# Seven-unit periods and a shared ring of banks in the attention stage of a two-layer fp32 kernel

## The reference, cut to what matters

```
q = _l2norm(q) * sm                 # sm = exp(min(scale_mul, log 100))
k = _l2norm(k)
scores = einsum('bhqd,bhkd->bhqk', q, k)
probs  = softmax(scores, axis=-1)
o      = einsum('bhqk,bhkd->bhqd', probs, v)
```

## Time and profile before

| what | us |
|---|---|
| three executions | 3588.06, 3583.96, 3587.75 |
| their median | 3587.75 |
| the profiled execution's own time | 3590.18 |
| span of the profiled execution, first to last instruction | 3588.4 |
| TensorE busy in the span | 3326.5 (93%) |
| VectorE, ScalarE, GpSimd busy | 2822.5, 2745.9, 2487.8 |
| granted TensorE clock, mean | 0.961 of full |

### The profile page before, as it was taken

One profiled execution on the slowest core, in us unless ns is written; L12 is line 12 of the kernel. 1 busy time (PEld: TensorE's weight loads), 2 busy tenths in 40 slices (PEclk: granted clock), 3 DMA queues, 4 the chain that ended last, 5 costly groups with the idle time before them and its releaser, 6 DMA issues.

```text
span 3588.4 us, 68227 instructions
## 1 busy us (share of the span) xinstructions
PE 3326.5 (93%) x22944; PEld 2607.0 (73%) x22944; DVE 2822.5 (79%) x2989; ACT 2745.9 (77%) x4725; POOL 2487.8 (69%) x1103
## 2 busy tenths in 40 slices
PE   7999999989799999997979999999798999999888
PEld 5778888864487888885357888888536888888643
DVE  2899999956299999994539999999445999999662
ACT  1989999933499999991449999998146999999523
POOL 1789999940098999992019999999103999999500
PEclk9999999998999999998889999999879999999989
DMA  3211212200112111110011111211002212111000
GB/s 125 86 61 54 69 54 67 66 24 1 51 60 67 57 66 61 60 66 12 1 63 60 61 62 61 66 56 60 12 1 74 65 55 65 54 60 54 24 12 6
DMA packets 56733, 186.83 MB, mean 52 GB/s; under 512 B 6577, under 2 KB 12721, under 8 KB 55473
## 3 DMA queue, kind: packets, MB, share of 16 engines
q1 hardware_dynamic: 56370, 182.26, 15.1%
HBM read 179.08 MB, written 3.16 MB: 51 GB/s over the span
## 4 chain that ended last, share of the span: by engine, by line
POOL 46%; PE 25%; issue 24%; DVE 3%; DMA 1%; ACT 0%; POOLq 0%; SPq 0%; DVEq 0%; ACTq 0%
POOL states L502 44%; PE bank L951 5%; PE bank L836 3%; PE bank L827 2%; PE bank L972 2%; PE bank L876 2%; PE bank L983 2%; PE bank L1025 2%; PE bank L828 1%; PE bank L750 1%; PE bank L776 1%; POOL part L485 1%; PE bank L939 1%; DVE states L1177 0%; PE bank L920 0%
## 5 line engine op out<-in xcount | busy, mean ns | idle before, releaser
L502 POOL TENSOR_TENSOR states<-states,c_rows 128x1024 f32<-128x1024 f32 x1024 | 2401.7, 2381 | 614.4 <-DMA c_rows<-c_spill 322.0
L1177 DVE TENSOR_TENSOR_SCAN states<-decay,bank 128x512 f32<-128x512 f32 x2048 | 2337.7, 1201 | 151.3 <-PE bank L828 105.7
L614 ACT ACTIVATE decay<-dt,a_log 128x512 f32<-128x512 f32 x2048 | 1305.9, 711 | 0.0
L836 PE MATMUL bank<-ident,states 128*128 128x128 f32 x8192 | 1240.5, 275 | 36.5 <-POOL states L502 13.0
L827 PE MATMUL bank<-ident,inflow_tok 128*128 128x128 f32 x6144 | 1068.7, 283 | 63.8 <-DVE states L1177 55.2
L608 ACT ACTIVATE inflow_tok<-dtx_tok,b_tok 128x512 f32<-128x512 f32 x1536 | 995.7, 713 | 134.3 <-PE bank L828 133.9
L836 PEld LDWEIGHTS bank<-ident,states 128*128 128x128 f32 x8192 | 952.4, 142 | 80.0 <-POOL states L502 77.5
L827 PEld LDWEIGHTS bank<-ident,inflow_tok 128*128 128x128 f32 x6144 | 687.5, 141 | 358.8 <-issue 126.0
L828 PE MATMUL bank<-b_diag,dtx_tok 128*128 128x128 f32 x4096 | 794.4, 276 | 0.0
L828 PEld LDWEIGHTS bank<-b_diag,dtx_tok 128*128 128x128 f32 x4096 | 621.1, 192 | 0.0
L1264 DVE TENSOR_REDUCE decay<-bank 128x1 f32<-128x512 f32 x256 | 166.4, 687 | 87.7 <-PE bank L951 86.6
(11 more groups left out here) (142 smaller groups left out, 1988.3 us busy)
## 6 DMA issues: line engine op xcount, KB each, us to landing
c_rows<-c_spill SPq DMA_DIRECT2D x256, 512.0 KB, 3.7
xproj_w<-in_xproj_w SPq DMA_DIRECT2D x32, 320.0 KB, 4.4
in_w<-in_in_w SPq DMA_DIRECT2D x16, 512.0 KB, 4.6
in_w<-in_fc_w SPq DMA_DIRECT2D x8, 512.0 KB, 5.3
xproj_w<-in_w SPq DMA_DIRECT2D x8, 512.0 KB, 5.0
xproj_w<-in_fc_w SPq DMA_DIRECT2D x4, 1024.0 KB, 4.7
y_gated<-in_mod_w SPq DMA_DIRECT2D x1, 2048.0 KB, 7.5
x_ahead<-in_x SPq DMA_DIRECT2D x4, 512.0 KB, 5.3
```

What stands on the lines that cost most here:

```text
L502: pool.tensor_tensor(pair, pair, c_row, ALU.mult).then_inc(weighed, 1)
L614: act.activation(decay[:, r % SLOTS * KI + k, :], dt[:, d, k, :], ACT.Exp, scale=a_neg[:, d, k, s:s + 1]).then_inc(decay_ready, 1)
L836: last = pe.matmul(banks[KI + t][:, k * P:(k + 1) * P], states[:, r % SLOTS * KI + k, t * P:(t + 1) * P], ident[:], is_transpose=True, sta ...
L1177: dve.tensor_tensor_scan(states[:, slot, time], decay[:, slot, time], banks[k % INFLOW_BANKS][:, time], 0.0, ALU.mult, ALU.add).then_inc(s ...
```

## The change

The stream is cut into 16 periods of four transposed units. In each of the first 11 periods three score units are woven in, in the order S T S T S T T, then comes the `weigh` of the period before, then at most one turn. The lead is 31 score units over seven banks (0 to 6). After the lead, score units go around banks 0 to 2 and transposed units around banks 3 to 6. The turned maxima and lanes no longer have a bank: each takes one slot in the ring of banks 0 to 2 in its turn (the first turn of maxima, inside the lead, uses bank 7). The copies of the turned maxima of groups 1 to 3 move from ScalarE to VectorE. `t_head` picks the head of a transposed unit so that neighbours again lie in different quarters. Nothing else in the program is changed, and the count of matmuls, reductions and exponentials is the same.

```diff
-LEAD = 22
+LEAD = 31
+LEAD_BANKS = 7
 S_BANKS = 3
-T_BANKS = 3
+T_BANKS = HG
+S_STEP = 3
+PERIODS = UNITS // HG
+S_PERIODS = (UNITS - LEAD) // S_STEP
+Q_MAX_PERIOD = {HG * g - 2: g for g in range(1, NG)}
+LANES_PERIOD = {HG * (g + 1) + 1: g for g in range(NG - 1)}
+TURN_PERIODS = sorted(list(Q_MAX_PERIOD) + list(LANES_PERIOD)) + [PERIODS]
...
+        def lead_last(bank):
+            return max(u for u in range(LEAD) if u % LEAD_BANKS == bank)
+        def score_slot(u):
+            n = u - LEAD
+            return n + sum(p < n // S_STEP for p in TURN_PERIODS)
+        def turn_slot(p):
+            return min(p + 1, S_PERIODS) * S_STEP + TURN_PERIODS.index(p)
+        def score_bank(u):
+            return banks[u % LEAD_BANKS] if u < LEAD else banks[score_slot(u) % S_BANKS]
+        def turn_bank(p):
+            return banks[turn_slot(p) % S_BANKS]
+        def t_head(v):
+            return (LEAD + v // HG * S_STEP + 2 + v % HG) % HG
...
-                q_max(0)
+                act.wait_ge(q_max_turned, b * NG + 1)
+                act.activation(q_t[:, 0, :], banks[7], ACT.Copy).then_inc(q_max_ready, 1)
...
-                    if g and at == HG:
+                    if g and at == HG - 1:
                         lanes(g - 1)
-                    if g + 1 < NG and at == STEPS - 3:
-                        q_max(g + 1)
...
+                def slot_free(x):
+                    if x < S_BANKS:
+                        pe.wait_ge(neg_ready, b * UNITS + lead_last(x) + 1)
+                        return
+                    owner = x - S_BANKS
+                    for k, p in enumerate(TURN_PERIODS):
+                        if turn_slot(p) == owner:
+                            if p in Q_MAX_PERIOD:
+                                pe.wait_ge(q_max_ready, b * NG + Q_MAX_PERIOD[p] + 1)
+                            else:
+                                pe.wait_ge(o_ready, b * NG + LANES_PERIOD[p] + 1)
+                            return
+                    for u in range(LEAD, UNITS):
+                        if score_slot(u) == owner:
+                            pe.wait_ge(neg_ready, b * UNITS + u + 1)
...
                 def scores(u):
-                    if u >= S_BANKS:
-                        pe.wait_ge(neg_ready, b * UNITS + u - S_BANKS + 1)
+                    if u >= LEAD:
+                        slot_free(score_slot(u))
+                    elif u >= LEAD_BANKS:
+                        pe.wait_ge(neg_ready, b * UNITS + u - LEAD_BANKS + 1)
...
                 def scores_t(v):
-                    g, kt, i = v // STEPS, v % STEPS // HG, v % HG
+                    g, kt, i = v // STEPS, v % STEPS // HG, t_head(v)
                     if v % STEPS == 0:
                         pe.wait_ge(q_max_ready, b * NG + g + 1)
-                    if v >= T_BANKS:
+                    if v < T_BANKS:
+                        pe.wait_ge(neg_ready, b * UNITS + lead_last(S_BANKS + v) + 1)
+                    else:
                         pe.wait_ge(probs_t_ready, b * UNITS + v - T_BANKS + 1)
...
                 for u in range(LEAD):
                     scores(u)
-                    if u == STEPS + S_BANKS - 1:
-                        turn_q_max(0)
-                for v in range(UNITS):
-                    if v + LEAD < UNITS:
-                        scores(v + LEAD)
-                    scores_t(v)
-                    g, at = v // STEPS, v % STEPS
-                    if v >= 2 * HG - 1 and v % HG == HG - 1:
-                        weigh((v - HG) // STEPS, (v - HG) % STEPS // HG)
-                    if g and at == STEPS // 2:
-                        turn_lanes(g - 1)
-                    if g + 1 < NG and at == STEPS - 3:
-                        turn_q_max(g + 1)
-                weigh(NG - 1, TT - 1)
-                turn_lanes(NG - 1)
+                    if u == STEPS + LEAD_BANKS - 1:
+                        turn_q_max(0, banks[7])
+                for j in range(PERIODS):
+                    v, u = j * HG, LEAD + j * S_STEP
+                    if j < S_PERIODS:
+                        scores(u)
+                        scores_t(v)
+                        scores(u + 1)
+                        scores_t(v + 1)
+                        scores(u + 2)
+                    else:
+                        scores_t(v)
+                        scores_t(v + 1)
+                    scores_t(v + 2)
+                    scores_t(v + 3)
+                    if j:
+                        weigh(j - 1)
+                    if j in TURN_PERIODS:
+                        slot_free(turn_slot(j))
+                        if j in Q_MAX_PERIOD:
+                            turn_q_max(Q_MAX_PERIOD[j], turn_bank(j))
+                        else:
+                            turn_lanes(LANES_PERIOD[j], turn_bank(j))
+                weigh(PERIODS - 1)
+                slot_free(turn_slot(PERIODS))
+                turn_lanes(NG - 1, turn_bank(PERIODS))
...
-                for u in range(UNITS):
+                for u in range(LEAD):
                     least(u)
-                    if u >= LEAD and (u - LEAD) // STEPS and (u - LEAD) % STEPS == STEPS // 2:
-                        divide((u - LEAD) // STEPS - 1)
-                for g in range(2, NG):
-                    divide(g)
+                for j in range(PERIODS):
+                    if j < S_PERIODS:
+                        for m in range(S_STEP):
+                            least(LEAD + j * S_STEP + m)
+                    if j in Q_MAX_PERIOD:
+                        g = Q_MAX_PERIOD[j]
+                        dve.wait_ge(q_max_turned, b * NG + g + 1)
+                        dve.tensor_copy(q_t[:, g, :], turn_bank(j)).then_inc(q_max_ready, 1)
+                    if j in LANES_PERIOD:
+                        divide(LANES_PERIOD[j], turn_bank(j))
+                divide(NG - 1, turn_bank(PERIODS))
```

More of the change, by code:

```diff
@@ L650, in batch @@
                     act.activation(to, banks[i], ACT.Copy).then_inc(qk_t_ready, 1)
-                def q_max(g):
-                    act.wait_ge(q_max_turned, b * NG + g + 1)
-                    act.activation(q_t[:, g, :], banks[6], ACT.Copy).then_inc(q_max_ready, 1)
                 def lanes(g):
@@ L945, in scores @@
                 def scores(u):
                     t, g, i = u % STEPS // HG, u // STEPS, u % HG
-                    if u >= S_BANKS:
-                        pe.wait_ge(neg_ready, b * UNITS + u - S_BANKS + 1)
+                    if u >= LEAD:
+                        slot_free(score_slot(u))
+                    elif u >= LEAD_BANKS:
+                        pe.wait_ge(neg_ready, b * UNITS + u - LEAD_BANKS + 1)
                     a = slice(i * LANE, (i + 1) * LANE)
-                    pe.matmul(banks[u % S_BANKS], q_t[a, g, t * P:(t + 1) * P], k_t[a, g, :], start=True,
+                    pe.matmul(score_bank(u), q_t[a, g, t * P:(t + 1) * P], k_t[a, g, :], start=True,
@@ L952, in scores, with turn_q_max @@
                               stop=True).then_inc(scores_mm, 1)
-                def turn_q_max(g):
+                def turn_q_max(g, to):
                     pe.wait_ge(neg_ready, b * UNITS + (g + 1) * STEPS)
-                    if g >= 2:
-                        pe.wait_ge(o_ready, b * NG + g - 1)
                     for t in range(TT):
-                        last = pe.transpose(banks[6][:, t * P:(t + 1) * P], qk_pad[:, t, g, :], ident[:])
+                        last = pe.transpose(to[:, t * P:(t + 1) * P], qk_pad[:, t, g, :], ident[:])
@@ L973, in scores_t, with weigh, turn_lanes @@
                               stop=True).then_inc(scores_t_mm, 1)
-                def weigh(g, kt):
-                    v = g * STEPS + kt * HG
-                    pe.wait_ge(probs_t_ready, b * UNITS + v + HG)
+                def weigh(j):
+                    g, kt = j // TT, j % TT
+                    pe.wait_ge(probs_t_ready, b * UNITS + (j + 1) * HG)
                     if g and kt == 0:
                         pe.wait_ge(lanes_ready, b * NG + g)
-                    for i in range(HG):
+                    for v in range(j * HG, (j + 1) * HG):
+                        i = t_head(v)
                         last = pe.matmul(banks[7][i * LANE:(i + 1) * LANE, :], v_ones[:, kt, g * HG + i, :],
-                                         probs_t[(v + i) % len(probs_t)], start=(kt == 0),
+                                         probs_t[v % len(probs_t)], start=(kt == 0),
                                          stop=(kt == TT - 1), tile_position=(0, i * LANE))
                     last.then_inc(pv_mm, 1)
-                def turn_lanes(g):
+                def turn_lanes(g, to):
                     pe.wait_ge(lanes_ready, b * NG + g + 1)
-                    if g == NG - 1:
-                        pe.wait_ge(o_ready, b * NG + g)
                     for t in range(TT):
-                        last = pe.transpose(banks[6][:, t * P:(t + 1) * P], o_lanes[:, g, t * P:(t + 1) * P], ident[:])
```

(7 more changed lines are left out.)

## The result

Four executions of the changed kernel have a median of 3529.15 us, four of the kernel before 3587.9. One of the changed kernel's four took 4454.76 us, at a mean granted clock of 0.674 where the others had 0.963 to 0.964; the other three lie between 3528.44 and 3529.55, and the ratio is theirs. It is 0.9835, with a 95% interval from 0.9822 to 0.9848: faster by some 59 us, against a forecast of 3532 (3518 to 3558). The profiled execution took 3529.55 us, its span is 3527.8.

What follows compares the result with a forecast made beforehand. Bank round trips were taken to bound the attention stage. 19.0 us to the loop plus 53.0 made 72.0 a stage, gaining 59.7, or 55.4 with one late clock fall: 3534.8 from 3590.2, so 3532 as median; range 3518 to 3558.

Steps and rivals of the forecast that it cites:

- The bound: Attention stage of the kernel before: the round trip of three banks (matmul, read, matmul) bounds it; loop period 3.98 us.
- Lead: First reduction to loop start: VectorE becomes the bound at 0.65 us a reduction; 19.0 us, nine score units more.
- TensorE is units ahead: Inside the lead: the reason why `turn_q_max(0)` and the exponential's table load would cost nothing.
- Periods 0 and 1: Loop start at half clock: period 0 takes 4.5 us, period 1 takes 0.6 above a warm one.
- Warm periods: Periods 1 to 10: seven units in two rounds, 1.95 us, plus `weigh` 1.00; 2.95 us each if no bank is late.
- third-round rival: Scored periods: a late score slot or row quarter forces a third round; 3573 us, half of it 3552; chance 0.08.
- rival of dearer rounds: Scored periods: each of the two rounds takes 0.3 us longer, 24 us in all; 3556 us; chance 0.06.
- Turns: Ends of periods 2, 5, 6, 9 and 10: four transposes each, 0.59 us, 3.0 us a stage.
- wait at the end of period 10: Turn of group 3's maxima needs the reduction of that period's own last score unit: 0.2 us.
- Periods 11 to 15: Transposed units only: periods alternate between 2.06 and 3.34 us, 12.9 in all; last `weigh` waits 1.3, takes 1.0.
- late fall: Section behind the score units: one clock fall to 1.2 GHz kept among the four stages, giving 4.3 us back.
- slower rival: Periods 1 to 10: the clock falls, a period takes 5.8 us; 3648 us with all ten cold; chance 0.04.

Runs made afterwards that it cites:

- e3: The changed kernel with three banks for the transposed units instead of four, order and turns unchanged: 3614.0 us.
- e2: The changed kernel with three banks instead of seven in its lead of 31 units (first turn moved too): 3567.5 us.
- e1: The kernel before with its lead of 22 score units over seven banks (first turn moved too), loop unchanged: 3574.7 us, ratio 0.9962 to the kernel before.
- e9: The kernel before with six banks instead of three for transposed units in the 22 steps without score units: 3582.3 us, ratio 0.9984.
- e4: The changed kernel with transposed unit v on head v mod 4, so neighbours often share a row quarter: 3541.2 us.
- e7: The changed kernel with seven filler matmuls (128 x 512, never read) in the lead's first 21 units, one behind every third: 3528.4 us.
- e10: The changed kernel with the order S S S T T T T in a period instead of S T S T S T T: 3547.3 us.
- e12: e11 with a filler matmul (128 x 512, never read) behind every fourth score unit of the lead: 3505.3 us, ratio 0.9773.
- e11: The changed kernel with a lead of 28, its turn at the end, twelve scored periods, six banks for transposed units behind them: 3517.1 us, ratio 0.9807.

## Why the prediction was right, point by point

**The bound.** The bank round trips were the bound. e3 gives one of them back and the gain is gone; e2 gives back another and 38 us of 59 are gone. In the kernel before, two of the three parts taken singly bring only 14 us (e1) and 6 us (e9), with falls of the clock against them.

**Lead.** Forecast 19.0 us from the first reduction to the loop, measured 18.7. Two terms were off and nearly cancelled: a reduction costs 0.60 in an unbroken row (13.84 for 23), not 0.65, and `turn_q_max(0)` was costed at nothing but costs the gap of 1.02. "TensorE is units ahead" was true of its stream, not of the array: the score units issued before the turn last until 848.12, the turn runs from 848.05 to 849.16 at half clock, and the next score unit starts at 849.10.

```profile
835.18 12.94 PE L993 MATMUL bank<-dtx_tok,dt 32*128 32x512 f32 x46 [0.78 <-DVE dtx_tok L1306]
848.05 1.11 PE L1000 MATMUL bank<-ident,decay 128*128 128x128 f32 x4
849.10 4.92 PE L993 MATMUL bank<-dtx_tok,dt 32*128 32x512 f32 x16
```

That the sum came out within 0.3 us is luck.

**Periods 0 and 1.** From the first loop unit to the first `weigh` forecast 4.5 + 2.55, measured 6.9 (854.94 to 861.83). The clock was back 24.6 us after the first reduction, as before (24.6).

**Warm periods.** 2.95 forecast, 2.92 measured. Two rounds for seven units, with no bank late, even behind turns. The third-round rival did not occur; e4 shows that it would have, by 0.84 in four periods, with other heads, and by the wait that the rival names: the turned slot with its slack of 0.2 us. The rival of dearer rounds falls with the 1.92 us of seven units, and with it the Trainium skill's factor of 3.07 (TensorE: Matmul & The Clock Gate, Part 3): here four units cost the time of one.

**Turns.** 0.59 each: from 864.75 to 868.26 is 3.51 = 2.92 + 0.59. The wait at the end of period 10 is 0.16 (890.49 + 1.00 to 891.65), forecast 0.2.

**Periods 11 to 15.** From `weigh` at 893.30 to the last at 906.38 it is 13.08; forecast 3.34 + 2.06 + 3.34 + 2.06 + 2.3 = 13.1. The last two are split differently (2.66 and 1.69), since the turn of period 13 delays what follows.

**The late fall.** The one event of the forecast that did not come. The forecast kept one late fall of the clock (4.3 us) among four stages; there was none. Stage by stage the sum without it was 0.9 too long, 3.6 in all. Stages gained 63.3 against 59.7 (55.4 with the fall), and what is not the stage took 2.7 longer, which the forecast had at nothing and no run explains. So 3529 against 3532 is closer than the parts are.

**The slower rival.** TensorE is the bound now and half clock would count in full, but the clock stayed at 1.00 from 864 to the end of the first stage, and as long in the other three. Across the kernels the falls have a pattern. Of sixteen profiled stages with three banks for the transposed units (before, e1, e3, e9), eight lost the clock in their last part, and three more (e9) right behind it. Of forty with four banks in the scored periods, none did (e7 lost it once a stage, at the start of the loop). All of these stages come from one profiled execution a kernel. The Trainium skill, same page, "A second HAM failure mode: psum-queue depth-cycling", blames short idle times between groups of matmuls that cycle through banks; the pattern agrees, the exact trigger is not shown, since e9 fell with six banks at the end, and only e3 has three banks with the new order.

## What to carry to other kernels

When an engine cycles through n banks, write down the round trip (matmul, signal, read, signal) and divide by n; if that is more than the slowest engine's own time for a unit, banks are the bound, and it pays to share them by moving rare users (turns, copies) into the ring. A unit whose quarter is taken lets later ones pass (e4); a unit that waits for another engine holds up all behind it (e4, e10). So put one that may wait for a signal late in a round, and fill the quarters before it. Where an engine other than TensorE sets the pace of a stretch, a few idle matmuls there can hold the clock up for the next one, as long as they fit beside that engine (every fourth unit here, not every third) and end close to the next one (argued).

## What the runs showed of the hardware that was not expected

- A round of four units of 32 rows costs what one costs, 1.12 us (this the rows of before had), and seven units 1.92.
- The clock's late falls go with the number of transposed banks: in 8 of 16 stages with three transposed banks in the last part, in 0 of 40 with four. e1 scatters from 3566.7 us (mean granted clock 0.965) to 3589.7 (0.954), while four executions of e12 lie between 3503.0 and 3506.3.
- Six filler matmuls of 128 x 512 in 15.2 us of lead kept the clock at its upper level, where in e11, without them, it was at half for 17.1 us from 841.1 on.
- A transpose behind row-tiled matmuls starts as they end (848.05, 848.12). At half clock that holds the stream up long enough for VectorE to empty seven banks (a gap of 1.02), at full clock the gap is 0.35 (e7).
- A matmul whose quarter is taken is passed by later ones in other quarters (e4, 868.48). One that waits for a semaphore holds up all behind it (e4, 875.79), 0.84 us a period.
